# Filler products on TensorE in the thin slots of a slot-planned transformer kernel, with some planner constants moved

## The reference

```
x = x + 0.5 * ffn(layernorm(x))                 # 128x128 weight plus a rank-32 correction
x = x + attn0(layernorm(x))                     # l2-normed q, k; two rounds: state = softmax(state k) v
x = x + 0.5 * ffn(layernorm(x))
x = x + 0.5 * moe(layernorm(x))                 # 8 experts, top 2, and one shared: silu(x w1) * (x w3) @ w2
x = x + attn1(layernorm(x))                     # block mask, softmax(q k / sqrt(8)) v
x = x + 0.5 * moe(layernorm(x))
```

## Time and profile before

| | |
|---|---|
| median of three runs | 3592.15 us (3590.73 to 3599.85) |
| the profiled execution's own time | 3591.33 us |
| its span, first to last instruction | 3589.5 us |
| mean granted TensorE clock | 0.923 of full speed |
| TensorE (PE) busy | 3211.0 us, 89% |
| VectorE (DVE) busy | 2401.4 us, 67% |
| ScalarE (ACT) busy | 2074.8 us, 58% |
| GpSimd (POOL) busy | 1214.9 us, 34% |

### The profile page before, as it was taken

How to read it: one execution, slowest core, us unless ns; L and a number is a source line. 1 busy time by engine, 2 the same in 40 slices (tenths; PEclk the granted TensorE clock), 3 DMA queues, 4 the chain that set the end, 5 groups by cost and what they waited for, 6 DMA issues and landing times. The chain is left out here.

```text
span 3589.5 us, 53603 instructions
## 1 busy us (share of the span) xinstructions
PE 3211.0 (89%) x19094; PEld 1589.9 (44%) x19094; DVE 2401.4 (67%) x5281; ACT 2074.8 (58%) x2689; POOL 1214.9 (34%) x2291
## 2 busy tenths in 40 slices
PE   4789798889999999999999999999999999998986
PEld 2224343344444444444444444444444544444554
DVE  1627475667867676786767677786767678676672
ACT  2455465556666666666666666666666666664432
POOL 3223223242342424243342425243342425223321
PEclk6769698789999999999999999999999999999996
DMA  1000000010100111101000110000011100000110
GB/s 40 1 18 14 27 8 4 31 31 28 34 5 34 31 34 31 34 28 31 28 10 34 31 34 31 31 31 23 15 31 34 31 34 29 30 31 4 57 33 33
DMA packets 81496, 96.79 MB, mean 27 GB/s; under 512 B 50544, under 2 KB 68400, under 8 KB 81104
## 3 DMA queue, kind: packets, MB, share of 16 engines
q1 hardware_dynamic: 81232, 93.35, 8.1%
HBM read 82.76 MB, written 4.78 MB: 24 GB/s over the span
## 5 line engine op out<-in xcount | busy, mean ns | idle before, releaser
L785 ACT ACTIVATE probs<-ps 128x1024 f32<-128x1024 f32 x1536 | 1574.6, 1025 | 1114.9 <-PE ps L654 1100.6
L1016 DVE TENSOR_REDUCE negmax<-ps 128x2 f32<-128x1024 f32 x1024 | 1248.8, 1219 | 513.7 <-PE ps L691 498.6
L654 PE MATMUL ps<-qT,kT 32*128 32x512 f32 x3072 | 810.1, 522 | 173.5 <-ACT probs L785 128.3
L671 PE MATMUL ps<-probs,v 128*32 128x512 f32 x6144 | 893.4, 656 | 0.1
L654 PEld LDWEIGHTS ps<-qT,kT 32*128 32x128 f32 x3072 | 300.0, 191 | 1067.1 <-ACT probs L785 721.4
L1233 POOL TENSOR_TENSOR xe<-xT_m,G 128x512 f32<-128x512 f32 x288 | 366.5, 1275 | 1051.8 <-PE ps L726 1004.5
L726 PE MATMUL ps<-xe,w_sb 128*128 128x256 f32 x2304 | 660.8, 412 | 16.0 <-POOL xe L1233 8.1
L691 PE MATMUL ps<-kT,qT 32*128 32x512 f32 x2048 | 541.0, 523 | 90.5 <-DVE negmax L1016 74.6
L726 PEld LDWEIGHTS ps<-xe,w_sb 128*128 128x128 f32 x2304 | 403.6, 194 | 194.8 <-issue 137.3
L1073 DVE SCALAR_TENSOR_TENSOR th<-th,ps 128x256 f32<-128x256 f32 x576 | 237.3, 412 | 207.7 <-ACT th L815 202.8
L815 ACT ACTIVATE th<-ps 128x256 f32<-128x256 f32 x576 | 221.2, 384 | 176.6 <-PE ps L726 158.8
(11 more groups left out here) (167 smaller groups left out, 2514.1 us busy)
## 6 DMA issues: line engine op xcount, KB each, us to landing
G<-gates_dram SPq DMA_DIRECT2D x96, 768.0 KB, 6.1
maxrow<-negmaxT SPq DMA_DIRECT2D x512, 2.0 KB
v<-v_tok SPq DMA_DIRECT2D x256, 18.0 KB, 1.9
X<-in_x SPq DMA_DIRECT2D x16, 256.0 KB, 3.0
out<-X SPq DMA_DIRECT2D x16, 256.0 KB, 2.3
w_sb<-in_w SPq DMA_DIRECT2D x1, 1152.0 KB, 7.0
w_sb<-in_w SPq DMA_DIRECT2D x1, 576.0 KB, 9.0
gates_dram<-gT SPq DMA_DIRECT2D x32, 18.0 KB
```

What stands on the lines that cost most here:

```text
L654: nc.tensor.matmul(ps[:, B_ST + h, :], kT[a][rows, g * S + kc * P:g * S + (kc + 1) * P], qT[a][rows, g * S:(g + 1) * S], start=True, stop= ...
L671: ins = nc.tensor.matmul(ps[ROWS * j:ROWS * (j + 1), B_UT, :], v[:, at:at + ROWS], probs[:, n % QUADS, j, :], start=(kc == 0), stop=(kc == ...
L785: nc.scalar.activation(probs[:, quad % QUADS, j:j + 2, :], ps[:, B_ST:B_ST + 2, :], ACT.Exp).then_inc(sem["exp_done"], 1)
L1016: nc.vector.tensor_reduce(negative[:, tc, 2 * half:2 * half + 2], ps[:, B_SM:B_SM + 2, :], AX_X, ALU.max, negate=True).then_inc(sem["sm_re ...
```

## The change

Five things change.

1. `close()` gets a loop that runs when a slot's side work has been placed: in slots 0 to 1699 it sums `USE` (columns of full-array work that each step stands for) of this slot and the one before, and as long as that is below 4600, the load with one more `warm` stays at or below 0.9, and the bank that comes free first is free by plan, it adds a `warm`. (The loop tests `use` before each one, but `taken` grows with it, and `warm` itself counts 1024.)
2. `warm` is now two products of the identity with the identity, 128x128 each, written over a free side bank. Nothing reads them and they signal nobody; TensorE waits in `take_side` for the bank's last reader. The plan has 220 of them: 128 in slots 0 to 300, 92 from slot 1506 on, none between.
3. `PV_AT` goes from 3.8 to 3.6, so `pv` now stands ahead of the side work of its slot. `OVER` goes from 1.33 to 1.35, `UNIT1` from 1.95 to 1.65 and `P1_AT` from 69 to 63.
4. Lags: on ScalarE `m_gu` 0.6 to 1.0; on VectorE `m_gu` 1.8 to 2.0, `turn` 1.6 to 1.4, `uts` 0 to 0.4, `p0_qkv` and `ffn_y` 0.6 to 1.0.
5. `m_gt` is placed no earlier than 0.1 behind the last `m_xe` of the MoE run before.

```diff
-PV_AT = 3.8
+PV_AT = 3.6
-O0_AT, MOE0_AT, UNIT0, P1_AT = 4, 30, 1.75, 69
-O1_AT, MOE1_AT, UNIT1 = 84.5, 80, 1.95
+O0_AT, MOE0_AT, UNIT0, P1_AT = 4, 30, 1.75, 63
+O1_AT, MOE1_AT, UNIT1 = 84.5, 80, 1.65
...
-WARM = ()
+WARM_UNTIL, WARM_NEED, WARM_FULL = 1700, 4600, 0.9
+USE = {**{n: 1024 for n in "ffn_xt p0_xt p1_xt o_t m_xt p0_op p1_op turn warm".split()}, "ffn_y": 2048, "o_y": 2048,
+       "p0_qkv": 1536, "p1_qkv": 1536, "m_gu": 2048, "m_down": 2304, "fold": 1536, "st": 256, "sm": 256, "pv": 2048}
-FULL, OVER = 1.0, 1.33
+FULL, OVER = 1.0, 1.35
...
-    "act": {**{n: HOP for n in "st ffn_xt p0_xt p1_xt o_t m_xt p0_op p1_op m_gt m_gu".split()}, "p1_op": 1.0, "p0_op": 1.2},
+    "act": {**{n: HOP for n in "st ffn_xt p0_xt p1_xt o_t m_xt p0_op p1_op m_gt m_gu".split()}, "p1_op": 1.0, "p0_op": 1.2, "m_gu": 1.0},
-            "m_gu": 1.8, "turn": 1.6, "p1_qkv": 1.0, "sm": 0.6},
+            "m_gu": 2.0, "turn": 1.4, "p1_qkv": 1.0, "sm": 0.6, "uts": 0.4, "p0_qkv": 1.0, "ffn_y": 1.0},
...
+            extra = 0
+            while 0 <= slot < WARM_UNTIL and load.get(slot, 0) + COST["warm"] <= WARM_FULL:
+                use = sum(USE.get(m[2], 0) for m in taken if slot - 1 <= m[0] < slot + 1)
+                if use >= WARM_NEED:
+                    break
+                pos, bank = slot + min(load.get(slot, 0), 0.9), min(range(SIDES), key=lambda k: ends[k])
+                if pos < ends[bank] + 0.15:
+                    break
+                self.use[("warm", slot, extra)] = bank, uses[bank]
+                taken.append((pos, len(self.marks) + slot, "warm", (slot, extra)))
+                load[slot] = load.get(slot, 0) + COST["warm"]
+                extra += 1
...
-                nc.tensor.matmul(take_side(("warm", i))[:, 0:HALF], id_sb[:], w13_sb[:, 0, :, :], start=True, stop=True)
+                bank = take_side(("warm", slot, i))
+                for c in range(2):
+                    nc.tensor.matmul(bank[:, c * P:(c + 1) * P], id_sb[:], id_sb[:], start=True, stop=True)
```

More of the change, by code:

```diff
@@ L135, in place @@
                 pos = max(pos, placed[other] + gap)
+            if name == "m_gt":
+                runs = [m[3] for m in taken if m[2] == "m_stats"]
+                n = runs.index(args)
+                if n:
+                    ahead = ("m_xe",) + runs[n - 1] + (EX - 1,)
+                    if ahead not in placed:
+                        return None
+                    pos = max(pos, placed[ahead] + 0.1)
             if name in SIDE_EVENTS:
@@ L151, in place @@
                     self.use[key] = bank, uses[bank]
-                    uses[bank] += name != "warm"
+                    uses[bank] += 1
                     first[key[:-1]] = bank
@@ L298, in timeline @@
         t.at(end, "store", b, behind=(("m_down", b, 1, TC - 1, 1), 1.5))
-    for i, at in enumerate(WARM):
-        t.at(at, "warm", i)
     return t.close()
@@ L545, in take_side, with warm @@
                 return side_bank(key)
-            def warm(n, i):
-                nc.tensor.matmul(take_side(("warm", i))[:, 0:HALF], id_sb[:], w13_sb[:, 0, :, :], start=True, stop=True)
+            def warm(n, slot, i):
+                bank = take_side(("warm", slot, i))
+                for c in range(2):
+                    nc.tensor.matmul(bank[:, c * P:(c + 1) * P], id_sb[:], id_sb[:], start=True, stop=True)
             def turn_chunks(key, blocks):
@@ L739, in m_down @@
                     ins.then_inc(full_signal(key), 1)
-            play("pe", dict(fold=fold, ffn_xt=ffn_xt, ffn_y=ffn_y, p0_xt=p0_xt, p0_qkv=p0_qkv, p0_op=p0_op, st=st, pv=pv, turn=turn,
+            play("pe", dict(warm=warm, fold=fold, ffn_xt=ffn_xt, ffn_y=ffn_y, p0_xt=p0_xt, p0_qkv=p0_qkv, p0_op=p0_op, st=st, pv=pv, turn=turn,
                       sm=sm, o_t=o_t, o_y=o_y, m_xt=m_xt, m_logits=m_logits, m_gt=m_gt, m_gu=m_gu, m_down=m_down, p1_xt=p1_xt, p1_qkv=p1_qkv, p1_op=p1_op))
```

## The result

The changed kernel takes 3557.25 us in the median (3551.46 to 3560.05, four runs), the kernel before 3592.28 us (3590.73 to 3599.85). The ratio is 0.9903, 95% interval 0.9878 to 0.9928: 35 us less, where 63 were forecast. The time lies in the stated range of 3490 to 3570 us, but 29 us above the forecast of 3528 us and outside 3495 to 3552 us, the range that the forecast's own case had.

What follows compares the result with a forecast made beforehand. The prediction took TensorE at half speed to bound the first turns, and TensorE at full clock the middle. First turns -55, end -1 and middle -7 us made -63 us, to 3528 us; stated range 3490 to 3570 us.

Steps and rivals of the forecast that it cites:

- the forecast's own case: Whole kernel: fillers lift the clock in the first turns; 3528 us, own range 3495 to 3552 us, chance 0.68.
- What bounds the first turns: Slow stretches of turns 0 to 3: TensorE works at half speed; fillers lift the clock, -55 us.
- The comparison with the stretch at 690 us: Slots with two warm look to TensorE like that stretch, clock 1.00, so slots should last 1.75 to 2.11 us.
- The filler's price: Each warm, two products, takes 0.46 us at the full clock or 1.04 us at half.
- The end: From the last L1 window on: window, chain and last MoE together give -1 us.
- The chain: Steps from o_y to m_gt behind the last window: 13.8 us with fillers, 1.5 us longer than before.
- The last MoE: Fillers among the 18 m_gu and before the first m_down cost up to 6 us; faster first products give -1.5 us.
- The -7 for the last window: Last L1 window, 3504 to 3536 us: its 12 exponentials speed up to 1.75 us each, saving 7 us.
- The middle turns: Twelve turns: swapping pv and side work costs +0.3 us a turn, VectorE's order gives -0.9; together -7 us.
- rival 2: Middle turns pay: exposed copies cost 0.6 us each, VectorE's order gives nothing; +36 us, 3571 us, chance 0.08.
- 1 (rise in part): First turns: transposes or dependent steps keep half speed, gain at most 30 us; 3561 us, chance 0.14.
- 3 (slower): Fillers don't lift the clock and each warm takes 1.04 us: 3657 us, chance 0.06.

Runs made afterwards that it cites:

- e5: Kernel before plus fillers in slots 0 to 400 alone, old positions and lags, with the m_gt rule: 3538.78 us, ratio 0.9839.
- e4: Changed kernel with PV_AT back at 3.8, so pv stands behind the side work; new lags stay: 3541.58 us, ratio 0.9858.
- e8: As e5, with fillers also in slots 1600 to 1627, the last attention windows: 3536.85 us, ratio 0.9847.
- e2: Fillers as in the change, every position and lag as in the kernel before; the m_gt rule stays: 3546.38 us, ratio 0.9875.
- e12: The changed kernel measured again, unchanged, on the chip of e9 and e10: 3554.77 us, ratio 0.989.
- e1: Changed kernel without any fillers, all its positions and lags kept: 3605.55 us, ratio 1.0042.
- e3: Changed kernel with fillers in slots 0 to 400 alone, none in the last turns: 3548.32 us, ratio 0.9878.
- e6: Fillers as in the change, old lags and positions, only pv ahead of side work (PV_AT 3.6): 3553.42 us, ratio 0.9879.
- e9: e8 plus 60 fillers in turns 4 to 15, before sm in slots 10, 11 and 19 of the turn: 3528.09 us, ratio 0.9812.
- e10: Changed kernel plus the same 60 fillers as e9, before sm in slots 10, 11 and 19 of turns 4 to 15: 3512.74 us, ratio 0.9782.
- e7: As e5, but each filler is four transposes of the identity instead of two products: 3547.41 us, ratio 0.9866.

## Why the prediction came out as it did

**What bounds the first turns: right.** TensorE at half speed was the bound, and raising the clock gave -53.9 us, where the text had -55; the other profiles with the same fillers have -48 to -61 us (e5, e4), so that the two agree to 1 us is luck. The comparison with the stretch at 690 us held: in turn 3 the 25 exponentials take 1.88 us each, well between the text's 1.75 and 2.11 us. In turns 0 and 1 it is 97 in 206 us, 2.12 us each, at the upper bound; the text had named the stalls of these turns, and e5 shows 15.4 us of idle time before `st` and 11.1 before `sm` from 60 to 290 us.

**The filler's price: right.** The 52 records before `m_gt`, 13 fillers, took 6.05 us, 0.47 us each, where 0.46 was worked out.

**The end: right in size, with terms that were off.** The chain was right (13.8 us forecast, 13.5 measured, 12.4 without fillers). The last MoE was 1.2 us short (+4.5 forecast; 23.5 against 17.8 us, +5.7), since the first products still ran at half speed. The -7 for the last window was too large: 3 to 6 us, by e8 and by e2. And 13 fillers stand between slot 1506 and the last window, for which the sum had no term; from the start of turn 15 to the last twelve slots it takes 439.4 us in the changed kernel and 434.5 in e12, where e1 and e3, without them, take 433.8 and 433.5. By the cuts the fillers of the end cost 2 to 9 us (the change and e12 against e1 and e3; 6.3 in e2 against before), where -1 was forecast, and the new order gives 3.5 back (e1). The changed kernel's two profiles have +4.1 and -1.3 us for both together.

**The middle turns: the step that failed.** The text had -7 us, from "TensorE's sum is the same in either order, so the swap costs nothing as long as neither waits", and measured was +14 and +19 us over eleven of the twelve turns. The whole new order costs that (e1, +20 us), and e4 and e6 put it down to the swap at least in part. TensorE's sum was not the same: it is busy for 10.8 us longer with the same records, 18.4 in e1, while its idle time stays within 4 us. It wasn't the exposed copy of rival 2 either. The list of waits of TensorE over the middle turns (us in total, times, longest) shows it, before and then changed:

```profile
PE ps L691 <- DVE negmax L1016: 43.5, 71, 1.3
PE ps L654 <- ACT probs L785: 34.3, 121, 1.1
```

```profile
PE ps L716 <- DVE negmax L1041: 57.3, 78, 1.4
PE ps L679 <- ACT probs L810: 25.6, 112, 0.5
```

The wait for Exp went down, by 8.7 us, and by another 12.1 before L691; the wait for VectorE's maxima went up by 13.8, and new waits for GpSimd came to 13.2 us, so that the idle time as a whole hardly moved. What the step left out is that the same products take longer where the clock is down, and that a swap changes how often it falls behind a wait: half-speed time is 105.6 us before, 143.9 after and 166.6 in e1, and half of what it grew by, 19 and 31 us, covers the loss of 14 and 20. I named the clock only as a bonus on less waiting. I also took +0.3 us a turn out of a range of 0 to +3 for the exposed copies, without a reason. The other half of the step, that VectorE's new order saves waiting (-0.9 us a turn), didn't come out: e4, with the new lags and `pv` behind, waits 56.1 us for the maxima (before 43.5) and has 149.2 us of idle time in all (before 146.6). Between e9 (old order) and e10 the wait for the maxima falls from 38.1 to 29.0 us, 0.8 us a turn. No run has these lags alone with fillers at the waits, so whether that is theirs stays open.

**Rivals.** 1 (rise in part): no; its reason, that transposes don't count, fell with e7. The Trainium skill says this of transposes in "TensorE: Matmul & The Clock Gate", "Part 4: PE-mode transpose"; for the float32 transposes of this kernel the measurement decides otherwise. 2 (the middle pays): in its sign and size nearly, 2280 and 2285 us for what took 2266, and not by its mechanism. 3 (slower): no. The rule about long idle gaps that the Trainium skill has in "TensorE: Matmul & The Clock Gate", "HAM oscillation — how this bites in real kernels", doesn't explain the kernel before: from 238 to 253 us its TensorE waits 1.2 us at most and runs at clock 0.50. In the middle turns the clock falls behind waits of 1.1 to 1.3 us.

**The range** held in part by luck. The forecast's own case ended at 3552 us; 3557 us lies in the part that was added for rivals 1 and 2, and neither mechanism is what happened.

**Left open.** Why `pv` ahead of the side work makes the clock fall more often in slot 19 was not settled: in the stretch shown above the order of TensorE's steps is the same in both kernels, and no run moves `pv` at single places. Nor is it shown how much of the loss is the swap's and how much the lags', and no run has fillers near slot 52.

## What to carry to other kernels

Read the granted clock of each stretch before you read busy shares: an engine that is 80% busy at half speed may be short of work, and products nobody reads can be a cheap fix, as long as they stand where the engine waits and not in a chain or in a full stage. Short waits of about a microsecond matter where the clock falls behind them; 60 fillers placed right in front of such waits gave 42 us in the changed kernel and 9 in the old order. And judge a change of order by TensorE's busy time, its idle time and its half-speed time, each by itself: here the order lost 15 us as a whole although its waits hardly grew. Last, look at which execution was profiled: a stage of the slowest run of one kernel against the fastest of another shows more than the order does.

## What the runs showed of the hardware that was not expected

- In a stream where TensorE is busy 94% of the time (191.91 of 205 us) the clock falls behind some waits of about a microsecond and not behind others as long: behind those of 1.3 us in slot 11 in 8 to 11 of 11 turns, behind those of 1.1 us in slot 19 of the kernel before in 5, behind those of 1.2 us that end before a transpose near slot 92 in none of that kernel. These last are here:

```profile
PE ps L554 <- ACT kT L776: 13.2, 11, 1.2
```

- With two fillers (1.16 us) in the waits of slots 11 and 19 the clock fell behind none of these 22 waits in e10.
- Float32 transposes of the identity lift the clock as products do: 0.92 against 0.91, from 0.67.
- The gain is not proportional to the filler: one product gave clock 0.88 from 60 to 290 us, two gave 0.91 (0.67 without).
- With fillers the clock is at the upper level in the last chain (`o_y` 1.16 us, 2.00 without), and from `o_y` to `m_gt` it is still 1 us longer (13.5 against 12.4).
